# Waiting for the low half in the middle of a product, and joined VectorE operations, in a two-layer transformer block

## The chip, the cores and the metric

The kernel runs on one core of one Trainium2 chip. The metric is the time of one execution on the device in microseconds (us). Before the change the median of three runs was 2668.15 us (2664.14 to 2672.86).

## The reference

The input x has 8 batches of 1024 rows of 256 numbers, all float32. Two blocks follow each other, each behind a layer normalisation that is scaled and shifted per batch (adaLN), and each added back to x with a gate.

```python
h = layernorm(x) * (1 + ca) + sa
x = x + ga * attn(h)          # q, k, v per head group; rope; causal softmax over 1024 rows
h = layernorm(x) * (1 + cb) + sb
x = x + gb * ffn(h)           # two layers:
#   qkv = shift(h) @ wqkv ; q, k = l2norm(q) * qs, l2norm(k) * ks ; rotary + xpos
#   o = local attention: 8 heads of 64, windows of 128 rows, each sees itself and the window before
#   h = h + o @ wo ; n = layernorm(shift(h)) * lg + lb
#   h = h + (a * gelu(g)) @ w2 + b2, with a, g = split(n @ w1 + b1)
```

`shift` moves the second half of the columns down by one row. The rotary step is `t * cos + swap(t) * sin`, where `swap` exchanges the two halves of the 64 columns of a head.

## The kernel before

**Halves.** To keep the accuracy of float32 with float16 products, most operands are stored as a float16 high half and a float16 low half (what is left over). A product is then three matrix products: high times high, high times the other's low, and low times the other's high. The helper `mm3` (lines 160 to 162) issues the three for one block of the contraction: `a[0] b[0]`, `a[0] b[1]`, `a[1] b[0]`. The high half is written by ScalarE (a copy to float16) and the low half after it by VectorE, or by GpSimd for the first normed rows, as the float32 source less the high half.

**Pieces and their order.** The work is cut into pieces, named by a letter or two and numbers for batch or window. A table of planned times (`BEGIN`, `EDGE`, `ONCE`) gives, by sorting, one fixed order of pieces for each engine; the table is not changed. Engines run their own list in order and meet only at semaphores. A piece waits at its start (`wait_ge`) and signals at its end. Every TensorE piece also takes its PSUM banks (`claim`), which waits until the piece that had the bank before is read out. A batch takes about 325 us; the order overlaps the end of one batch's second layer with the start of the next batch's first attention.

**TensorE pieces that the change touches.** `pj` projects 128 normed rows to q, k, v (two blocks of 384 columns, six products, 64 pieces). `sc` forms the causal scores of 128 rows against all rows so far (per bank of 512 columns six products, and one with the mask; 64 pieces). `E` is a third of a window's qkv (six products of 512 columns, 384 pieces). `J` is the output projection of a window (twelve products of 256 columns, 128 pieces). `Wg` and `Wa` are a block of 128 hidden columns for 512 rows, gate and value (six products of 512 columns, 192 and 160 pieces). Each waited at its start for the low half of its rows. The high halves come from ScalarE's pieces `hh` (line 674), `qc` (689), `dh` (723), `nh` (731) and `oh` (809), the low halves from `hl` (GpSimd, line 1316) and VectorE's `ql` (967), `dl` and `nl` (1021) and `ol` (1104). Piece `Y`, the second MLP product, isn't changed: it waits for each block of the hidden rows just before that block's three products.

At the end of a layer the order is: `J` of the last windows, the residual (`jr`, line 1110), the DMA of the rows shifted by one (`xs`), the statistics (1117 to 1122), GpSimd's inverse root (294, 296), the normed rows (1131, 1133), their transposes (407), `nh`, `nl`, and the first `Wg` of those rows.

**VectorE pieces that the change touches.** `rp` (lines 943 to 946) multiplies the q and k columns of a projected tile, read from PSUM, with cos and sin; GpSimd adds the two parts (1321). `x0` and `x1` (1051, 1059) form the cos and sin products of a window's rotary step; GpSimd adds them (1343). `nm` (1084, 1090) takes the inverse of four row sums of the window softmax and scales two of the four heads' probabilities; ScalarE's `na` (791) scales the other two.

Of the kernel before, what the change touches and what calls it, by code (L numbers as in the profile page):

```python
# [18 lines left out]
ALU = mybir.AluOpType  # L19
# [3 lines left out]
P = 128  # L23
EPS = 1e-5
BIG = 1.0e30
BATCH, SEQ, DIM = 8, 1024, 256
NT = SEQ // P
NC = DIM // P
# [3 lines left out]
DEPTH = 2  # L32
HEADS, DH = 8, 64
INNER = HEADS * DH
# [5 lines left out]
HQ = P // 2  # L40
KW = 192
# [5 lines left out]
def adaln_kernel(nc, x, w_q, w_k, w_v, wqkv, q_scale, k_scale, wo, ln_g, ln_b, w1, b1, w2, b2,  # L47
# [3 lines left out]
    with ExitStack() as ctx:  # L51
# [172 lines left out]
        def at(*piece):  # L224

            return rank[piece]
# [61 lines left out]
        def pw_at(f, q, i):  # L288

            return HQ + (HQ + KW) * (4 * f + 2 * q + i)  # L290
# [9 lines left out]
        with block:  # L300
# [100 lines left out]
            def _(pe):  # L401
# [9 lines left out]
                for piece in ORDER["pe"]:  # L411
# [10 lines left out]
                    elif k == "pj":  # L422
                        b, t = ids
                        pe.wait_ge(s_hl, at("hl", b, t // 2))
                        if b == 0 and t == 0:
                            pe.wait_ge(s_bdl, 1)
                        bk = claim(pe, *piece)
                        for c in range(NC):
# [13 lines left out]
                    elif k == "sc":  # L442
                        b, i = ids
                        pe.wait_ge(s_ql, at("ql", b, i))
                        if b == 0 and i == 0:
                            pe.wait_ge(s_masks, 1)
                        bk = claim(pe, *piece)
                        n = (i + 1) * P
                        for kb in range((n + 511) // 512):
                            w = min(512, n - kb * 512)  # L450
                            for c in range(NC):
                                mm3(pe, ps[:, bk + kb, 0:w], [q[:, c, 0, i * P:(i + 1) * P] for q in QK1],
                                    [q[:, c, 1, kb * 512:kb * 512 + w] for q in QK1], c == 0, c == 1)
                        last = pe.matmul(ps[:, bk + i // 4, (i % 4) * P:(i % 4 + 1) * P], id_b[:],
# [32 lines left out]
                    elif k == "E":  # L487
                        n, s = ids
                        L, w = divmod(n, NT)
                        pe.wait_ge(s_dl, at("dl", L, w // 2))  # L490
                        if L < DEPTH and w < 2:
# [3 lines left out]
                        for c in range(NC):  # L495
                            a = w * P + (1 - c)
                            last = mm3(pe, ps[:, bk, :], [q[:, c, a:a + P] for q in ht],
                                       [q[:, L % DEPTH, c, s * INNER:(s + 1) * INNER] for q in wqkv_p], c == 0, c == 1)
                        last.then_inc(s_qkv, 1)
# [68 lines left out]
                    elif k == "J":  # L568
                        n, = ids
                        pe.wait_ge(s_ol, at("ol", n))  # L570
                        if n in (0, NT):
                            pe.wait_ge(s_do, at("do", n // NT))
                        bk = claim(pe, *piece)
                        for c in range(4):
                            last = mm3(pe, ps[:, bk, 0:DIM], [q[:, c, :] for q in ot],
                                       [q[:, n // NT % DEPTH, c, :] for q in wo_p], c == 0, c == 3)
                        last.then_inc(s_wo, 1)
                    elif k in ("Wg", "Wa"):
                        L, g, j = ids
# [8 lines left out]
                        for c in range(NC):  # L588
                            last = mm3(pe, ps[0:m, bk, :], [q[:, L % DEPTH, c, 2 * j + i, 0:m] for q in w1_p],
                                       [q[:, c, a:a + 512] for q in ht], c == 0, c == 1)  # L590
                        last.then_inc(s_w1 if i else s_w1g, 1)
# [293 lines left out]
            def _(dve):  # L885
                for piece in ORDER["dve"]:
# [39 lines left out]
                    elif k == "rp":  # L926
# [6 lines left out]
                        elif b:  # L933
                            dve.wait_ge(s_add, at("ad", last_n(b)))
                        bk = bank["pj", b, t]
                        for c in range(NC):
                            src = ps[:, bk + c, 0:2 * P].rearrange("p (s i e) -> p s i e", s=2, e=2)
                            a = ra[:, t % 2, c].rearrange("p s (i e) -> p s i e", e=2)
                            bb = rb[:, t % 2, c].rearrange("p s (i e) -> p s i e", e=2)
                            cs = cos_t[:, t, c, :].unsqueeze(1).broadcast_to((P, 2, 64))  # L940
                            sn = sin_t[:, t, c, :].unsqueeze(1).broadcast_to((P, 2, 64))
# [90 lines left out]
                    elif k in ("x0", "x1"):  # L1032
# [22 lines left out]
                        if l == 0 and w == 0:  # L1055
                            dve.wait_ge(s_qkt, at("qt", L // DEPTH, NT - 1))
                        for e in range(2):
                            lo, hi = slice(32 * e, 32 * e + 32), slice(32 - 32 * e, 64 - 32 * e)
                            last = dve.tensor_tensor(m2[:, :, :, lo], raw[:, :, :, hi], sn[:, :, :, lo], ALU.mult)  # L1059
                        last.then_inc(s_m, 1)  # L1060
                    elif k == "tm":
# [16 lines left out]
                    elif k == "nm":  # L1078
# [815 lines left out]
```

## Time and profile before

| | |
|---|---|
| median of three runs | 2668.15 us (2664.14 to 2672.86) |
| the profiled execution | 2665.09 us, its span 2663.3 us |
| mean granted TensorE clock | 0.985 |
| TensorE busy | 2533.0 us |
| VectorE busy | 2274.1 us |
| ScalarE busy | 1932.2 us |
| GpSimd busy | 1300.6 us |

The profile comes from one execution. Busy times are the union of an engine's instructions; the ends of matrix products are modelled, so that a product's listed duration is longer than the distance to the next one's start. The distance between starts shows the pace. A wait names the engine whose signal ended it. PE is TensorE, PEld its weight loads, DVE VectorE, ACT ScalarE, POOL GpSimd.

### The profile page before, as it was taken

To read this page: it belongs to the slowest core of one execution; us is meant where nothing else is said; L and a number is where in the kernel's file an instruction comes from. 1 tells how busy PE (TensorE), PEld (TensorE's weight loads), DVE (VectorE), ACT (ScalarE), POOL (GpSimd) and SP (SyncE) were. 2 spreads that over 40 slices of the span, in tenths; PEclk is the share of its full clock that TensorE was granted. 3 is DMA by queue.
4 is the path that set the end of the run, shared out by engine and by line. 5 is a ranking of instruction groups with operands and counts; after the bars stand their busy time and mean duration, and the time that the engine had idled before them with its cause. 6 is when DMAs were issued, how large, how long until landed. Compare 5 with 4: busy or idle time off the path is not lost. (4 is left out here: it accounts for less than half of the span.)

```text
span 2663.3 us, 71937 instructions
## 1 busy us (share of the span) xinstructions
PE 2533.0 (95%) x25566; PEld 1726.5 (65%) x25566; DVE 2274.1 (85%) x6823; ACT 1932.2 (73%) x4782; POOL 1300.6 (49%) x953
## 2 busy tenths in 40 slices
PE   7899989999899998999989999999999999989997
PEld 4566666667566665676656666666766666666675
DVE  8897889878898788987889878898889978799785
ACT  3598856878468784778747787587874888648884
POOL 2364534655355553555435554365544555445552
PEclk7999999999999999999999999999999999999999
DMA  5000010000100000000000000000000000000000
GB/s 190 21 7 8 5 43 2 9 6 8 39 3 9 6 16 30 4 10 4 18 29 5 9 5 20 25 6 8 6 19 25 6 8 6 19 25 6 7 6 21
DMA packets 51026, 46.49 MB, mean 17 GB/s; under 512 B 11530, under 2 KB 47980, under 8 KB 50548
## 3 DMA queue, kind: packets, MB, share of 16 engines
q1 hardware_dynamic: 50004, 40.78, 5.0%
q8 instruction: 213, 3.49, 0.5%
q14 instruction: 137, 1.12, 0.1%
q10 hardware_dynamic: 672, 1.10, 0.1%
HBM read 25.06 MB, written 8.42 MB: 13 GB/s over the span
## 5 line engine op out<-in xcount | busy, mean ns | idle before, releaser
L780 ACT ACTIVATE ar_b<-ar_b,small 128x192 f32<-128x192 f32 (+1 forms) x1024 | 445.3, 437 | 80.7 <-DVE small L1073 79.8
L1343 POOL TENSOR_TENSOR ar_c<-ar_c 128x1024 f32<-128x1024 f32 x128 | 302.7, 2365 | 284.0 <-DVE ar_c L1059 283.2
L1339 POOL TENSOR_TENSOR small<-small,neg_half 128x16 f32<-128x16 f32 x128 | 380.6, 2974 | 115.0 <-DVE small L1031 112.0
L1073 DVE CUSTOM_DVE_ANT_0 ar_b<-ps,mask_t,small 128x192 f32<-128x192 f32 x896 | 318.9, 411 | 27.0 <-PE ps L529 26.8
L1358 POOL TENSOR_TENSOR mlp<-mlp 128x512 f16<-128x512 f32 x160 | 198.0, 1243 | 204.2 <-ACT mlp L835 203.6
L160 PE MATMUL ps<-wqkv_hi,ht_hi 128*128 128x512 f16 x768 | 292.9, 381 | 0.0
L162 PE MATMUL ps<-wqkv_hi,ht_lo 128*128 128x512 f16 x768 | 291.6, 380 | 0.0
L161 PE MATMUL ps<-wqkv_lo,ht_hi 128*128 128x512 f16 x768 | 291.6, 380 | 0.0
L160 PE MATMUL ps<-ht_hi,w_hi 128*128 128x512 f16 (+1 forms) x704 | 269.1, 382 | 11.3 <-DVE ht_lo L1021 11.3
L162 PE MATMUL ps<-ht_hi,w_lo 128*128 128x512 f16 (+1 forms) x704 | 268.3, 381 | 0.0
L161 PE MATMUL ps<-ht_lo,w_hi 128*128 128x512 f16 (+1 forms) x704 | 268.1, 381 | 0.0
L563 PE MATMUL ps<-ar_b,ar_a 128*64 128x128 f32 x3840 | 239.8, 276 | 0.5 <-DVE ar_b L1098 0.3
L294 POOL TENSOR_SCALAR stats<-stats 128x2 f32<-128x2 f32 x128 | 30.4, 237 | 426.6 <-DVE stats L1122 327.7
L563 PEld LDWEIGHTS ps<-ar_b,ar_a 128*64 128x64 f32 x3840 | 207.2, 137 | 30.1 <-issue 20.5
L1149 DVE SCALAR_TENSOR_TENSOR mlp<-ps,bias,mlp 128x512 f32<-128x512 f32 x192 | 142.3, 748 | 75.1 <-PE ps L162 33.7
L529 PE MATMUL ps<-ar_a 64*64 64x64 f32 (+2 forms) x5536 | 196.9, 282 | 2.9 <-ACT ar_a L770 2.8
L791 ACT ACTIVATE ar_b<-ar_b,rsw 128x192 f32<-128x192 f32 (+1 forms) x512 | 192.8, 440 | 7.4 <-DVE rsw L1084 7.1
L780 ACT ACTIVATION_READ_ACCUMULATOR ar_b<-ar_b,small 128x1 f32 x1024 | 193.1, 189 | 0.0
L1098 DVE COPY ar_b<-ps 128x512 f32<-128x512 f32 (+1 forms) x256 | 160.1, 648 | 35.7 <-PE ps L547 35.4
L529 PEld LDWEIGHTS ps<-ar_a 64*64 64x64 f32 x5536 | 153.7, 133 | 40.0 <-issue 22.8
L160 PE MATMUL ps<-w_hi,mlp 128*128 128x256 f16 x640 | 175.3, 274 | 0.2 <-POOL mlp L1358 0.2
L161 PE MATMUL ps<-w_lo,mlp 128*128 128x256 f16 x640 | 175.1, 274 | 0.0
(197 smaller groups left out, 6911.7 us busy)
## 6 DMA issues: line engine op xcount, KB each, us to landing
xu<-in_L_attn_x_dram SPq DMA_DIRECT2D x32, 256.0 KB, 2.9
out_dram<-xu SPq DMA_DIRECT2D x64, 128.0 KB, 2.5
rows<-xu SPq DMA_DIRECT2D x128, 63.5 KB
mlp<-in_L_ffn_wqkv_dram SPq DMA_DIRECT2D x2, 1536.0 KB, 6.6
modb<-mod_rows SPq DMA_DIRECT2D x8, 384.0 KB, 4.3
rows<-in_L_ffn_w_dram SPq DMA_DIRECT2D x2, 1364.0 KB, 10.3
rows<-xu SPq DMA_DIRECT2D x112, 0.5 KB
ar_b<-in_L_wmod_dram SPq DMA_DIRECT2D x2, 768.0 KB, 7.1
```

The source lines that it names most:

```text
L160: pe.matmul(o, a[0], b[0], start=start, stop=False)
L161: pe.matmul(o, a[0], b[1], start=False, stop=False)
L162: return pe.matmul(o, a[1], b[0], start=False, stop=stop)
L529: last = pe.matmul(ps[HQ * half:HQ * half + HQ, bk[q], i * KW + o:i * KW + o + m], QT[r:r + HQ, n % 2, hp, HQ * half:HQ * half + HQ], KT[r ...
L563: last = pe.matmul(ps[64 * q:64 * q + 64, bk, (h // 2) * P:(h // 2 + 1) * P], V[:, (n - 1 + kb) % 4, h * DH:(h + 1) * DH], PTW[:, f, q, 2 ...
L780: last = act.activation(pw, pw, ACT.Exp, bias=mnw[:, n % 2, h:h + 1], scale=-1.0, accum_out=smw[:, n % 2, h:h + 1])
L791: last = act.activation(pw, pw, ACT.Copy, scale=rsw[:, n % 2, h:h + 1])
L1073: last = dve.tensor_tensor_reduce(out=PW[:, pw_at(f, q, i) + c:pw_at(f, q, i) + KW], in0=ps[:, bk, i * KW + c:(i + 1) * KW], in1=mask, sca ...
L1098: dve.tensor_copy(PTW[:, f].rearrange("p x k n -> p (x k) n")[:, c - 1:8:c, 0:HQ], ps[:, bank["H", n, f, 0], :].rearrange("p (k n) -> p k ...
L1339: pool.tensor_tensor(rinv[:, n % 4, :], ssm[:, n % 2, :], neg_half[:, 0:16], ALU.pow).then_inc(s_rinv, 1)
L1343: pool.tensor_tensor(M1[:, n % 2, :], M1[:, n % 2, :], M2, ALU.add).then_inc(s_add, 1)
L1358: pool.tensor_tensor(lo, UB[r, v % 2, :], hi, ALU.subtract).then_inc(s_ul, 1)
```

## The change

In the six kinds of pieces the wait for the low half moves behind the high products, and a wait for the high half stands at the start. The products are the same in number and operands, in another order: first those that need only the high half of the rows, for all blocks of the contraction, then the others. In `pj`, `E`, `J`, `Wg` and `Wa` two thirds of the products come first, in `sc` a third, since there both operands have a late low half.

In VectorE's pieces, operations of one kind on neighbouring parts become one operation with a longer access pattern. `rp` goes from eight operations of 128 elements per partition to three of 256 and two of 128. `x1` goes from two operations of 512 to one of 1024, which reads the halves of each head in swapped order by a negative step. `nm` goes from two operations of 192, each with a per-row scalar (`tensor_scalar`), to one of 384 with the two scalars as a second tensor, repeated by a step of zero (`tensor_tensor`). The regular windows have 192 elements a head, the first window of a sequence 128.

```diff
                     elif k == "pj":
-                        pe.wait_ge(s_hl, at("hl", b, t // 2))
+                        pe.wait_ge(s_hh, at("hh", b, t // 2))
...
                         for c in range(NC):
-                            h = [q[:, c, 1 + t * P:1 + (t + 1) * P] for q in ht]
-                            w = [q[:, c, :, :].rearrange("p s n -> p (s n)") for q in bd_p]
-                            last = mm3(pe, ps[:, bk + c, 0:3 * P], h, w, True, True)
+                            for i in range(2):
+                                pe.matmul(ps[:, bk + c, 0:3 * P], ht[0][:, c, 1 + t * P:1 + (t + 1) * P], w[c][i],
+                                          start=(i == 0), stop=False)
+                        pe.wait_ge(s_hl, at("hl", b, t // 2))
+                        for c in range(NC):
+                            last = pe.matmul(ps[:, bk + c, 0:3 * P], ht[1][:, c, 1 + t * P:1 + (t + 1) * P], w[c][0],
+                                             start=False, stop=True)
                         last.then_inc(s_proj, 1)
...
                     elif k == "sc":
-                        pe.wait_ge(s_ql, at("ql", b, i))
+                        pe.wait_ge(s_qk, at("qc", b, i))
...
+                        for low in range(2):
+                            if low:
+                                pe.wait_ge(s_ql, at("ql", b, i))
+                            for kb in range((n + 511) // 512):
+                                w = min(512, n - kb * 512)
+                                for c in range(NC):
+                                    for q_half, k_half in (((0, 1), (1, 0)) if low else ((0, 0),)):
...
                     elif k == "J":
-                        pe.wait_ge(s_ol, at("ol", n))
+                        pe.wait_ge(s_oh, at("oh", n))
...
                         for c in range(4):
-                            last = mm3(pe, ps[:, bk, 0:DIM], [q[:, c, :] for q in ot],
-                                       [q[:, n // NT % DEPTH, c, :] for q in wo_p], c == 0, c == 3)
+                            for i in range(2):
+                                pe.matmul(ps[:, bk, 0:DIM], ot[0][:, c, :], wo_p[i][:, n // NT % DEPTH, c, :],
+                                          start=(c == 0 and i == 0), stop=False)
+                        pe.wait_ge(s_ol, at("ol", n))
+                        for c in range(4):
+                            last = pe.matmul(ps[:, bk, 0:DIM], ot[1][:, c, :], wo_p[0][:, n // NT % DEPTH, c, :],
+                                             start=False, stop=(c == 3))
...
                     elif k in ("Wg", "Wa"):
-                        pe.wait_ge(s_nl, at("nl", L, 2 * g + 1))
+                        pe.wait_ge(s_nh, at("nh", L, 2 * g + 1))
...
                    elif k == "rp":
...
+                        for e in range(2):
+                            dve.tensor_tensor(a[:, :, :, :, e], src[:, :, :, :, e], cs, ALU.mult)
                         for c in range(NC):
...
-                            for e in range(2):
-                                dve.tensor_tensor(a[:, :, :, e], src[:, :, :, e], cs, ALU.mult)
-                            dve.scalar_tensor_tensor(out=bb[:, :, :, 0], in0=src[:, :, :, 1], scalar=-1.0, in1=sn,
+                            dve.scalar_tensor_tensor(out=bb[:, c, :, :, 0], in0=src[:, c, :, :, 1], scalar=-1.0, in1=sn[:, c],
                                                      op0=ALU.mult, op1=ALU.mult)
-                            last = dve.tensor_tensor(bb[:, :, :, 1], src[:, :, :, 0], sn, ALU.mult)
+                        last = dve.tensor_tensor(bb[:, :, :, :, 1], src[:, :, :, :, 0], sn, ALU.mult)
...
                    elif k in ("x0", "x1"):
...
-                        for e in range(2):
-                            lo, hi = slice(32 * e, 32 * e + 32), slice(32 - 32 * e, 64 - 32 * e)
-                            last = dve.tensor_tensor(m2[:, :, :, lo], raw[:, :, :, hi], sn[:, :, :, lo], ALU.mult)
-                        last.then_inc(s_m, 1)
+                        swap = raw.rearrange("p s h (e d) -> p s h e d", e=2)[:, :, :, ::-1, :]
+                        dve.tensor_tensor(m2.rearrange("p s h (e d) -> p s h e d", e=2), swap,
+                                          sn.rearrange("p s h (e d) -> p s h e d", e=2), ALU.mult).then_inc(s_m, 1)
...
                    elif k == "nm":
...
-                        for i in range(2):
-                            h = 4 * f + 2 * i
-                            pw = PW[:, pw_at(f, 0, i) + c:pw_at(f, 0, i) + KW]
-                            last = dve.tensor_scalar(pw, pw, rsw[:, n % 2, h:h + 1], None, ALU.mult)
-                        last.then_inc(s_pn, 1)
+                        pair = PW[:, pw_at(f, 0, 0) - HQ:pw_at(f, 0, 0) - HQ + 2 * (HQ + KW)].rearrange(
+                            "p (i k) -> p i k", i=2)[:, :, HQ + c:HQ + KW]
+                        scale = rsw[:, n % 2, 4 * f:4 * f + 4:2].unsqueeze(2).broadcast_to((P, 2, KW - c))
+                        dve.tensor_tensor(pair, pair, scale, ALU.mult).then_inc(s_pn, 1)
```

Piece `E` is changed as `J` is, with `dh` and `dl`; `Wg` and `Wa` have the weights on the other side, so their first products are `w1` high and `w1` low times the rows' high half.

## Rows read from the trace of the kernel before

**Rows 1.** The page: busy us (share of span) and instructions; shares of the chain

```profile
PE 2533.0 (95%) x25566; PEld 1726.5 (65%) x25566; DVE 2274.1 (85%) x6823; ACT 1932.2 (73%) x4782; POOL 1300.6 (49%) x953
...
PE 14%; DVE 3%; ACT 2%; issue 1%; DMA 0%; POOL 0%; POOLq 0%; DVEq 0%; ACTq 0%
```

**Rows 2.** Waits of TensorE, whole span: us in total, times, longest us

```profile
PE ps L160 <- POOL ht_lo L1316: 26.0, 17, 5.9
PE ps L160 <- DVE ar_a L967: 23.1, 16, 2.5
PE ps L160 <- DVE rows L1104: 16.7, 16, 1.4
PE ps L160 <- DVE ht_lo L1021: 11.3, 8, 1.4
```

**Rows 3.** The chain at the seam of two batches: start us, us, what

```profile
2289.92 0.70 DVE rows L1104
...
2295.36 0.70 DVE rows L1104
...
2298.09 5.15 DMA rows<-xu
...
2307.45 0.61 ACT ht_hi L731
...
2308.09 0.70 DVE ht_lo L1021
```

**Rows 4.** Timeline of TensorE: start us, us, operation, [idle before, releaser]

```profile
2339.65 0.34 PE L160 MATMUL ps<-ar_a 128*128 128x384 f16 x1 [2.52 <-DVE ar_a L967]
```

**Rows 5.** The chain in the first attention of the last batch

```profile
2328.97 0.40 DVE ar_c L943 x2
2329.37 0.20 DVE ar_c L944
...
2348.68 1.27 POOL ar_c L1321
```

**Rows 6.** Windows: us, busy us (instructions) of each engine, PEclk, DMA share, GB/s

```profile
2326.00:2350.00 24.00, 17.96 (x137) 12.93 (x135) 21.80 (x72) 8.68 (x16) 11.19 (x13) 1.00 0.21 67
...
2430.00:2500.00 70.00, 69.69 (x763) 48.92 (x763) 60.20 (x175) 54.63 (x139) 37.04 (x25) 1.00 0.03 9
...
1366.20:1376.40 10.20, 8.57 (x31) 4.67 (x29) 8.19 (x25) 2.62 (x6) 5.82 (x7) 0.50 0.28 97
```

**Rows 7.** Timeline of TensorE in piece Y, across a wait

```profile
1194.31 0.27 PE L162 MATMUL ps<-w_hi,mlp 128*128 128x256 f16 x1
1194.42 0.27 PE L160 MATMUL ps<-w_hi,mlp 128*128 128x256 f16 x1
```

**Rows 8.** Timeline of VectorE, three stretches

```profile
1404.56 1.23 DVE L1051 TENSOR_TENSOR ar_c<-ar_b,xp_t 128x1024 f32<-128x1024 f32 x1
1405.70 1.29 DVE L1059 TENSOR_TENSOR ar_c<-ar_b,xp_t 128x512 f32<-128x512 f32 x2
1406.91 1.28 DVE L974 TENSOR_TENSOR ar_b<-ps,ar_b 128x512 f16<-128x512 f32 x2
...
1502.08 0.55 DVE L1090 TENSOR_SCALAR ar_b<-ar_b,rsw 128x192 f32<-128x192 f32 x2
1502.54 0.42 DVE L1110 TENSOR_TENSOR xu<-ps,xu 128x256 f32<-128x256 f32 x1
...
1514.97 0.41 DVE L1110 TENSOR_TENSOR xu<-ps,xu 128x256 f32<-128x256 f32 x1
1515.30 1.28 DVE L1059 TENSOR_TENSOR ar_c<-ar_b,xp_t 128x512 f32<-128x512 f32 x2
```

**Rows 9.** Line 1090 alone: duration ns min/median/max, starts, forms

```profile
L1090 DVE TENSOR_SCALAR ar_b<-ar_b,rsw x512: 278/315/1194, 124.8 to 2614.0; 128x192 f32<-128x192 f32 x149, 128x128 f32<-128x128 f32 x22
```

More of the change, by code:

```diff
@@ L427, in _ @@
                         bk = claim(pe, *piece)
+                        w = [[q[:, c, :, :].rearrange("p s n -> p (s n)") for q in bd_p] for c in range(NC)]
                         for c in range(NC):
-                            h = [q[:, c, 1 + t * P:1 + (t + 1) * P] for q in ht]
-                            w = [q[:, c, :, :].rearrange("p s n -> p (s n)") for q in bd_p]
-                            last = mm3(pe, ps[:, bk + c, 0:3 * P], h, w, True, True)
+                            for i in range(2):
[5 more added lines that the diff above has]
+                                             start=False, stop=True)
                         last.then_inc(s_proj, 1)
@@ L448, in _ @@
                         n = (i + 1) * P
[L449 to L453, printed above, removed]
+                        for low in range(2):
[5 more added lines that the diff above has]
+                                    for q_half, k_half in (((0, 1), (1, 0)) if low else ((0, 0),)):
+                                        pe.matmul(ps[:, bk + kb, 0:w], QK1[q_half][:, c, 0, i * P:(i + 1) * P],
+                                                  QK1[k_half][:, c, 1, kb * 512:kb * 512 + w],
+                                                  start=(not low and c == 0), stop=(c == 1 and q_half == 1))
                         last = pe.matmul(ps[:, bk + i // 4, (i % 4) * P:(i % 4 + 1) * P], id_b[:],
@@ L489, in _ @@
                         L, w = divmod(n, NT)
-                        pe.wait_ge(s_dl, at("dl", L, w // 2))
+                        pe.wait_ge(s_dh, at("dh", L, w // 2))
                         if L < DEPTH and w < 2:
@@ L496, in _ @@
                             a = w * P + (1 - c)
-                            last = mm3(pe, ps[:, bk, :], [q[:, c, a:a + P] for q in ht],
-                                       [q[:, L % DEPTH, c, s * INNER:(s + 1) * INNER] for q in wqkv_p], c == 0, c == 1)
+                            for i in range(2):
+                                pe.matmul(ps[:, bk, :], ht[0][:, c, a:a + P],
+                                          wqkv_p[i][:, L % DEPTH, c, s * INNER:(s + 1) * INNER],
+                                          start=(c == 0 and i == 0), stop=False)
+                        pe.wait_ge(s_dl, at("dl", L, w // 2))
+                        for c in range(NC):
+                            a = w * P + (1 - c)
+                            last = pe.matmul(ps[:, bk, :], ht[1][:, c, a:a + P],
+                                             wqkv_p[0][:, L % DEPTH, c, s * INNER:(s + 1) * INNER],
+                                             start=False, stop=(c == 1))
                         last.then_inc(s_qkv, 1)
@@ L574, in _ @@
                         for c in range(4):
-                            last = mm3(pe, ps[:, bk, 0:DIM], [q[:, c, :] for q in ot],
-                                       [q[:, n // NT % DEPTH, c, :] for q in wo_p], c == 0, c == 3)
+                            for i in range(2):
+                                pe.matmul(ps[:, bk, 0:DIM], ot[0][:, c, :], wo_p[i][:, n // NT % DEPTH, c, :],
+                                          start=(c == 0 and i == 0), stop=False)
+                        pe.wait_ge(s_ol, at("ol", n))
+                        for c in range(4):
+                            last = pe.matmul(ps[:, bk, 0:DIM], ot[1][:, c, :], wo_p[0][:, n // NT % DEPTH, c, :],
+                                             start=False, stop=(c == 3))
                         last.then_inc(s_wo, 1)
@@ L588, in _ @@
                         for c in range(NC):
-                            last = mm3(pe, ps[0:m, bk, :], [q[:, L % DEPTH, c, 2 * j + i, 0:m] for q in w1_p],
-                                       [q[:, c, a:a + 512] for q in ht], c == 0, c == 1)
+                            for q in w1_p:
+                                pe.matmul(ps[0:m, bk, :], q[:, L % DEPTH, c, 2 * j + i, 0:m], ht[0][:, c, a:a + 512],
+                                          start=(c == 0 and q is w1_p[0]), stop=False)
+                        pe.wait_ge(s_nl, at("nl", L, 2 * g + 1))
+                        for c in range(NC):
+                            last = pe.matmul(ps[0:m, bk, :], w1_p[0][:, L % DEPTH, c, 2 * j + i, 0:m], ht[1][:, c, a:a + 512],
+                                             start=False, stop=(c == 1))
                         last.then_inc(s_w1 if i else s_w1g, 1)
```

10 lines of the change are left out of this document (5 added, 5 removed).

## The prediction

> **What bounds the kernel now.** I read the shares first: TensorE is busy 95% of the span and VectorE 85% [rows 1], so at most some 130 us of TensorE idleness can be won. The chain of waits comes next. It could be followed over the last 550 us, the last 21% of the span: 14 points of it are TensorE, 3 VectorE, 2 ScalarE [rows 1]. TensorE's own waits say what its idle time waited for, and the four longest are the four kinds of low half that the change moves: 26.0 us for GpSimd's `ht_lo`, 23.1 for `ar_a` (q and k of the first attention), 16.7 for `rows` (the window attention's output), 11.3 for `ht_lo` by VectorE, together 77.1 us [rows 2]. So the question is which of these are on the path that sets the end.
>
> Their counts fit a batch: 16 waits for `rows` are two in each of 8 batches, 8 waits for VectorE's `ht_lo` one each. The chain shows where these three stand, at the seam between two batches [rows 3]: at 2289.92 and 2295.36 it goes from ScalarE's high half of the output through VectorE's subtraction (0.70) into piece J, then through the 5.15 us of the shifted rows' DMA, and at 2307.45 from ScalarE's high half of the normed rows (0.61) through VectorE's subtraction (0.70) into the first Wg. Three times a batch, then, the low half is on the path and TensorE has nothing else in its queue that may go ahead.
>
> The other two kinds stand elsewhere. TensorE sits idle 2.52 us before a score piece at 2339.65 [rows 4], but there the chain runs on VectorE: the rotations from 2328.97 on are on it, and those whose sum GpSimd forms at 2348.68 [rows 5], and from 2326 to 2350 VectorE is busy 21.80 of 24 us against 17.96 for TensorE [rows 6]. In the middle of a batch nothing is idle: TensorE 69.69 of 70 us from 2430 to 2500 [rows 6].
>
> **The waits moved.** A piece that waited for the low half now waits for the high half, sends its high products and waits then. It wins the least of three: the wait itself, the time between the two halves, and the time of the products that go first. For J, eight of twelve products come first; products of 256 columns start 0.11 us apart [rows 7], so 0.87 us. For Wg they are four of six at 0.22 us, 0.86 us. Both exceed the subtraction of 0.70 plus its two hand-overs of some 0.02, so 0.72 is won whole, and the high half, made by ScalarE, is late next. The waits leave room for it: 11.3/8 = 1.41 us for Wg and 16.7/16 = 1.04 for J [rows 2], counted from the end of the product before, which the profile sets at 0.27 us though the next could start after 0.11 [rows 7], so another 0.16 is hidden in it. 3 x 0.72 x 8 batches = 17.3 us, all on the path.
>
> For pj, four of six products come first, 0.16 us each, 0.65 us; for a score piece only two of six (high times high), 0.33 us at the 384 columns of the longer wait; the other of the two waits per batch is 23.1/8 - 2.52 = 0.37 us. That is 17 x 0.65 + 8 x 0.33 + 8 x 0.37 = 17 us of TensorE's idle time, but it lies where VectorE sets the pace (or, for the pj at the seam, in front of the Wg whose high half comes no sooner for it). It returns as a longer wait for VectorE: I take 0, and up to 17 if VectorE isn't the bound there. The E, Wa and J pieces of the middle have waits too short for the list; TensorE is idle 0.31 us in 70 there [rows 6], so 8 batches hold under 8 us, and I take 1.
>
> What a wait in mid-product costs is seen in piece Y, which waits for each block of the hidden rows between two products: L162 at 1194.31, the wait, L160 at 1194.42, 0.11 us like everywhere [rows 7]. A wait already met costs nothing there. So the 992 waits that are added (64 pj, 64 sc, 384 E, 128 J, 352 Wg and Wa) are worth 0; the upper bound is a weight load exposed at each, 1726.5/25566 = 0.068 us [rows 1], 67 us. Behind a mid-product wait that is not met stands all of TensorE's queue, but it stood behind the same wait before, one piece earlier: no start moves back. Products, weight loads and bank claims stay the same in number.
>
> **The joined VectorE operations.** A rotation tile (64 of them) has eight operations of 128 elements, now five. Half of them take 0.80 us on the chain (0.40 for two, 0.20 for the third, as much for the fourth) [rows 5]; one of 256 elements out of PSUM takes 0.33 (L1110 at 1514.97 to the next start) [rows 8]. Three pairs at 0.40 become three at 0.33 to 0.34, so 0.19 a tile, 12 us of VectorE time. Four of a batch's eight tiles are on the chain (two around 2328.97, one ahead of 2348.68, one later; rows 5 show one half tile of the four); the others run beside stretches of the chain on TensorE and GpSimd. 4 x 0.19 x 8 = 6 us. Bounds: 0 and 12.
>
> The swapped halves (128 tiles): two operations of 512 take 1.21 us (1405.70 to 1406.91), one of 1024 takes 1.14 (1404.56 to 1405.70) [rows 8]: 0.07 x 128 = 9 us of VectorE time. VectorE has 3 of the chain's 21 points [rows 1], which gives 1.3 us; I take 1.3. Nothing in the trace reads with a negative step; if it ran at half rate, 1.07 x 128 = 137 us more.
>
> The normalisation (256 pairs): the two `TENSOR_SCALAR` of 192 elements take 0.46 us (1502.08 to 1502.54) [rows 8], 0.23 each. A two-tensor operation of 384 elements lies between 256 (0.33) and 512 (0.60) in rows 8, at 0.47. That is no gain although an operation falls away: I take 0, between -2 (128-wide tiles of the first windows) and +5. The reason is in the numbers: the two-tensor forms cost (0.60 - 0.33)/256 = 1.05 ns an element and 0.06 us fixed, by which 192 elements would take 0.26; the one-source form takes 0.23. The Trainium skill has the rule for it ("VectorE: DVE Perf Modes", section "Mode 2x_2P"): a one-source fp32 operation in SBUF may use both read ports and give two results a cycle, and a `tensor_tensor` cannot. The trace agrees in direction, 0.23 against 0.26. By the count of operations alone, without that rule, the joined form would save 0.06 x 256 = 15 us of VectorE time.
>
> The longest of these operations took 1.19 us, the median one 0.315 [rows 9], so some of them are held up. I put 0 on this, since the joined operation starts where the first of the pair did. The Trainium skill ("SBUF — State Buffer", section "Who interferes with whom") says that both forms, the two-port one and the one with two SBUF inputs, block against a GpSimd operation that reads SBUF; by it nothing changes but the length of the hold.
>
> **Sum.** 17.3 + 1 + 6 + 1.3 + 0 = 25.6 us. The profiled execution took 2665.1 us (its span is 2663.3), so 2639.5; the median of the runs shown, 2668.15, is 3.1 us above the profiled one, and on that scale I predict 2642.5.
>
> **The rivals.**
> (a) More than that. VectorE's relief (12 + 9 us) is all on the path and part of the 17 us of pj and scores comes through: 17 + 21 + 5 = 43 us, 2625. For it: VectorE is busy 21.80 of 24 us at the seam. Against it: half of the rotations are off the chain.
> (b) Given back. The three on-path savings are 5 us apart; if the shifted DMA or ScalarE's order holds one of the three and the rotations' gain goes into GpSimd's add (1.27 us, on the chain behind them), 12 us remain: 2656. For it: VectorE is busy there nearly throughout, and may be late next. Against it: the chain at the seam is serial, and each link waits for the one before.
> (c) The change doesn't shorten anything: a PSUM group left open in mid-product holds back what ran ahead before, or the next semaphore is late by as much. 0 us, 2668. Piece Y speaks against it.
> (d) Slower, by TensorE's clock. It is at half (0.50, the 1.2 GHz level) for 10.2 us from 1366.2, in the first attention of a batch, and at full speed in the middle of the last one [rows 6]. If the changed rhythm of short and split waits brings such a stretch to every batch where TensorE sets the pace, it costs 5.1 x 8 = 41 us: 2642 + 41 = 2683. It decides from 26 us on, that is from 6.5 us at half clock a batch. Against it: the waits get shorter, so TensorE is denser.
>
> **Chances.** Forecast 0.56 (its own range 2634 to 2650), (a) 0.12, (b) 0.15, (c) 0.09, (d) with a slow negative step or exposed weight loads beside it 0.08. A measurement of this kernel tells about 0.3%, 8 us, from no change. Faster by more than that: 0.56 + 0.12 + 0.14 = 0.82; same 0.10; slower 0.08. The range 2628 to 2661 leaves out about a tenth on either side.
>
> **What would show it.** In the changed profile: TensorE's wait for `rows` falls from 16.7 us towards 5 and turns into one for ScalarE's `rows`; the wait for VectorE's `ht_lo` falls from 11.3 by 5.8; those for `ht_lo` by GpSimd and for `ar_a` shrink, with idle time of about that size found elsewhere at the seam. Each seam gets some 3 us shorter, the middle keeps its length. VectorE's busy time falls by some 20 us, from the rotations and the swap and not from the normalisation, whose joined form shows 0.47 us to the next start. TensorE's busy time stays. I am wrong if the middle of a batch changes length, if a met mid-product wait shows a gap over 0.11 or 0.22 us, or if the seam does not shrink.

## The result, and the profile after

The changed kernel takes 2640.14 us (median of four runs, 2639.26 to 2644.93) against 2668.15 for the kernel before (2664.14 to 2672.86): ratio 0.990, 95% interval 0.9883 to 0.9917. That is 28.0 us less, with 25.6 predicted (2642.5 us). One run of the kernel before (2960.05 us) and the one profiled run of `order` (2949.09 us, mean granted clock 0.841) fell into a slower state and are left out of every comparison. Timed again beside its parts, the same change gave 0.9896 (0.9884 to 0.9909), 27 us. The profiled execution took 2644.93 us, span 2642.6, mean granted clock 0.983.

The page of the kernel after, busy us (share) and instructions:

```profile
PE 2536.8 (96%) x25566; PEld 1729.8 (65%) x25566; DVE 2258.1 (85%) x6247; ACT 1932.7 (73%) x4782; POOL 1303.9 (49%) x953
```

VectorE is busy 16.0 us less than in [rows 1], TensorE as before. TensorE's waits after (us in total, times, longest us), for [rows 2]:

```profile
PE ps L419 <- DVE ar_c L936: 12.8, 16, 4.1
PE ps L407 <- DVE rows L1159: 12.6, 16, 5.1
PE ps L461 <- DVE ar_a L995: 10.0, 8, 1.3
PE ps L431 <- ACT ht_hi L702: 9.1, 9, 4.7
PE ps L594 <- ACT rows L837: 5.6, 8, 0.7
PE ps L613 <- ACT ht_hi L759: 5.5, 8, 0.7
PE ps L461 <- ACT ar_a L717: 4.8, 7, 0.7
PE ps L565 <- DVE ar_b L1117: 4.8, 8, 0.6
...
PE ps L435 <- POOL ht_lo L1342: 3.9, 10, 0.8
```

`rows` went from 16.7 us to 5.6 and is now ScalarE's (line 837, before 809): 8 waits instead of 16. `ht_lo` of the first `Wg` (11.3) became ScalarE's `ht_hi` (5.5). The 26.0 for GpSimd's `ht_lo` became 9.1 and 3.9, the 23.1 for `ar_a` 10.0 and 4.8. In their place the transposes of normed rows (lines 419, 407) wait longer. And there is a new one: 0.6 us, eight times, for `ar_b` of line 1117, the normalisation that the change joins (`jw`, where it is not joined, has the same wait). These timelines of the last seam show where it stands. TensorE after (start us, us, operation, [idle before, releaser]), with J of window 14 at 2273.69 between the transposes `H` (line 565) and J of window 15 at 2279.08:

```profile
2273.03 0.71 PE L565 MATMUL ps<-id_f,ar_b 64*128 64x64 f32 x16
2273.69 0.28 PE L594 MATMUL ps<-wo_hi,rows 128*128 128x256 f16 x1
...
2275.77 0.71 PE L565 MATMUL ps<-id_f,ar_b 64*128 64x64 f32 x16 [0.60 <-DVE ar_b L1117]
...
2279.08 0.28 PE L594 MATMUL ps<-wo_hi,rows 128*128 128x256 f16 x1 [0.70 <-ACT rows L837]
...
2291.30 0.39 PE L613 MATMUL ps<-ht_hi,w_hi 128*128 128x512 f16 x1 [0.69 <-ACT ht_hi L759]
```

The same pieces before (the transposes `H` are line 547 there, J and `Wg` line 160):

```profile
2289.29 0.71 PE L547 MATMUL ps<-id_f,ar_b 64*128 64x64 f32 x16
2290.67 0.28 PE L160 MATMUL ps<-wo_hi,rows 128*128 128x256 f16 x1 [0.67 <-DVE rows L1104]
...
2292.08 0.71 PE L547 MATMUL ps<-id_f,ar_b 64*128 64x64 f32 x16
...
2296.11 0.28 PE L160 MATMUL ps<-wo_hi,rows 128*128 128x256 f16 x1 [1.42 <-DVE rows L1104]
...
2308.83 0.39 PE L160 MATMUL ps<-ht_hi,w_hi 128*128 128x512 f16 x1 [1.42 <-DVE ht_lo L1021]
```

VectorE after, same stretch, with the first rotation tile behind it:

```profile
2273.67 0.69 DVE L1130 TENSOR_TENSOR rows<-ps,rows 128x512 f16<-128x512 f32 x1 [0.49 <-ACT rows L837]
2274.54 0.18 DVE L1111 RECIPROCAL rsw<-small 128x4 f32<-128x4 f32 x1 [0.18 <-ACT ar_b L808]
2274.75 0.56 DVE L1117 TENSOR_TENSOR ar_b<-ar_b,rsw 128x384 f32<-128x384 f32 x1
2275.22 0.68 DVE L1124 COPY ar_b<-ps 128x512 f32<-128x512 f32 x1
...
2291.88 0.75 DVE L970 TENSOR_TENSOR ar_c<-ps,cos_t 128x256 f32<-128x256 f32 x2
2292.54 0.48 DVE L972 SCALAR_TENSOR_TENSOR ar_c<-ps,sin_t 128x128 f32<-128x128 f32 x2
2292.94 0.42 DVE L974 TENSOR_TENSOR ar_c<-ps,sin_t 128x256 f32<-128x256 f32 x1
2293.27 0.75 DVE L970 TENSOR_TENSOR ar_c<-ps,cos_t 128x256 f32<-128x256 f32 x2
```

GpSimd of the kernel after, and then the same two operations before (line 1342 is 1316 there):

```profile
2286.66 1.09 POOL L1342 TENSOR_TENSOR ht_lo<-ar_c,ht_hi 128x512 f16<-128x512 f32 x1 [4.86 <-ACT ht_hi L702]
2287.72 0.22 POOL L294 TENSOR_SCALAR stats<-stats 128x2 f32<-128x2 f32 x1
```

```profile
2302.97 1.09 POOL L1316 TENSOR_TENSOR ht_lo<-ar_c,ht_hi 128x512 f16<-128x512 f32 x1 [4.86 <-ACT ht_hi L674]
2304.54 0.22 POOL L294 TENSOR_SCALAR stats<-stats 128x2 f32<-128x2 f32 x1 [0.48 <-DVE stats L1122]
```

How the three savings of a seam fare. J of window 14 sends its high products 0.72 us sooner (1.38 us after the first `H` before, 0.66 now), but the second `H` behind it then waits 0.60 for the normalisation, which VectorE does only after the low half (2273.67) and, from 2274.54, behind ScalarE's exponential: from `H` to `H` it takes 2.79 us before and 2.74 after, so hardly anything passes. J of window 15 gains 0.72 (4.03 us behind `H` before, 3.31 now). Of this 0.2 is lost at the root (line 294): before, GpSimd sat idle 0.48 ahead of it; now `ht_lo` of the next batch stands in front and ends as the root starts. The first `Wg` passes its gain whole: from J of window 15 to it 12.72 us became 12.22, that is its 0.72 less the 0.2.

The windows of the kernel after, its middle and a stretch of the first attention (us, busy us and instructions of PE, PEld, DVE, ACT, POOL, PEclk, DMA share, GB/s), for the last two of [rows 6]:

```profile
2409.00:2479.00 70.00, 69.71 (x795) 49.93 (x794) 60.48 (x165) 55.51 (x145) 37.14 (x24) 1.00 0.04 10
2002.60:2009.40 6.80, 6.11 (x21) 3.31 (x20) 6.20 (x18) 2.52 (x6) 3.56 (x6) 0.50 0.23 81
```

The middle is as dense as before, and half clock still comes in the first attention.

To place the time I cut each batch at ScalarE's operations, which have the same number in every kernel: A, first attention, from the first copy of v to the last exponential; B to the output of window 5; C to window 13; D to the last `nh`; S to the next copy of v. Means over batches 2 to 7 in us, worked out from the traces; "half" is the time at a granted clock of 0.50, per batch.

```
kernel       A     B     C      D     S     sum     half in A   half in D, S
before      61.94 97.58 127.78 31.77 5.05  324.12   5.1         0.6
changed     60.72 97.52 127.73 31.21 4.05  321.23   5.1         0      (run "both")
waits       61.33 97.60 127.63 31.23 4.05  321.83   6.3         0
no_qkv      61.28 97.63 127.70 31.21 4.05  321.87   5.7         0
jw          62.57 97.63 127.69 31.21 4.05  323.15   7.4         0
pjsc        61.39 97.62 127.80 31.79 5.68  324.30   5.1         2.3
joins       61.26 97.54 128.37 31.79 5.33  324.29   2.8         1.1
nm_apart    60.86 97.34 127.74 31.22 4.05  321.21   5.7         0
waits_rp    61.08 97.79 127.64 31.24 4.05  321.80   6.8         0
order_swap  61.47 97.53 127.74 31.64 4.05  322.43   5.7         0
```

D and S together give 1.56 us a batch, A gives 1.22, B and C 0.1. Eight times that is 23.1 us; the first batch gives 1.3 more, which makes the 24.3 between the two profiled executions (2665.09 and 2640.79). The medians are 27 apart. S is 4.77 before in all but one batch; in that one (6.45) 3.4 us of it are at half clock. So 0.28 of the 1.56 is clock, and 1.28 is the moved waits.

The lengths at half clock differ between batches of one kernel, so means of A mix them. Batch by batch, A of the kernel before takes 60.9 us with no half clock, 61.8 with 3.4 us of it, 61.9 to 62.0 with 6.8 and 63.2 with 10.2; A of the changed kernel takes 60.5 with 3.4 and, but for one batch of 61.4, 60.9 to 61.0 with 6.8. The gain of A is therefore 1.0 to 1.3 us at like clock too.

### The profile page after: what moved, and what is told of

Same layout as the page of the kernel before. It is cut to its first block and busy times, and to the rows that moved or that the text cites. A ratio compares the mean times of both kernels' runs of the same rounds, so it can differ in the third digit from the quotient of the medians.

```text
span 2642.6 us, 71361 instructions
## 1 busy us (share of the span) xinstructions
PE 2536.8 (96%) x25566; PEld 1729.8 (65%) x25566; DVE 2258.1 (85%) x6247; ACT 1932.7 (73%) x4782; POOL 1303.9 (49%) x953
## 5 line engine op out<-in xcount | busy, mean ns | idle before, releaser
L514 PE MATMUL ps<-wqkv_hi,ht_lo 128*128 128x512 f16 x768 | 229.0, 380 | 0.0
L617 PE MATMUL ps<-ht_lo,w_hi 128*128 128x512 f16 (+1 forms) x704 | 210.0, 380 | 0.0
L160 PE MATMUL ps<-w_hi,mlp 128*128 128x256 f16 x640 | 174.7, 273 | 0.2 <-POOL mlp L1384 0.2
L162 PE MATMUL ps<-w_hi,mlp 128*128 128x256 f16 x640 | 174.5, 273 | 0.0
## 6 DMA issues: line engine op xcount, KB each, us to landing
rows<-xu SPq DMA_DIRECT2D x128, 63.5 KB
```

The costliest lines, as they stand in the source:

```text
L514: last = pe.matmul(ps[:, bk, :], ht[1][:, c, a:a + P], wqkv_p[0][:, L % DEPTH, c, s * INNER:(s + 1) * INNER], start=False, stop=(c == 1))
L617: last = pe.matmul(ps[0:m, bk, :], w1_p[0][:, L % DEPTH, c, 2 * j + i, 0:m], ht[1][:, c, a:a + 512], start=False, stop=(c == 1))
```

## The experiments

Each was timed in five rounds; ratios are to the kernel before, with 95% intervals.

**both**: the whole change again, as the yardstick for its parts.

> The whole change again, timed beside its parts. Theory S (the seam's chain, with TensorE's low-half waits on it, sets the gain): about 26 us faster than before, 2641 us, ratio 0.990. Theory V (VectorE's saved 20 us carry the gain) and theory C (stretches of TensorE at half clock that come and go) give the same number here; C expects runs that differ by several us from each other with the half-clock stretches that they hold.

2640.92 us, 0.9896 (0.9884 to 0.9909). The result repeats.

**waits**: only TensorE's waits moved, VectorE as before.

```diff
 (pj, sc, E, J, Wg, Wa as in the change; rp, x1, nm as before)
```

> Only TensorE's waits are moved (pj, sc, E, J, Wg, Wa); VectorE's operations stay apart. Theory S: two thirds of the gain or more, 16 to 20 us faster, 2649 us. By the changed profile each seam passes on only 1.3 of the 2.17 us that were predicted, so with 0.3 us from each middle some 13 us is the low end. Theory V: at most 5 us faster.

2647.47 us, 0.9924 (0.9912 to 0.9936): 20 of the 27 us.

**joins**: only the joined operations.

```diff
 (rp, x1, nm as in the change; all TensorE pieces as before)
```

> Only VectorE's operations are joined (rp, x1, nm); all TensorE waits stay as before. Theory S: 6 to 8 us faster, 2660 us (0.21 us for each of the four rotations per batch on the chain, and little from the swap and the normalisation). Theory V: 20 us faster, 2648.

2665.91 us, 0.9997 (0.9988 to 1.0005): a miss for both theories. Alone they gain 0.7 us a batch in A (0.1 to 0.4 where the time at half clock is alike: 60.47 against 60.87 with none) and lose 0.6 in C and 0.3 in S. S's loss is clock, in two batches instead of one; in the others S is 4.77 as before. C's loss comes at one spot of each batch. VectorE and GpSimd of `joins` (nm is line 1089):

```profile
1834.78 0.56 DVE L1089 TENSOR_TENSOR ar_b<-ar_b,rsw 128x384 f32<-128x384 f32 x1
...
1836.62 0.35 DVE L1129 TENSOR_SCALAR rows<-xu,stats 128x128 f32<-128x128 f32 x1 [0.61 <-POOL stats L296]
```

```profile
1834.79 0.62 POOL L294 TENSOR_SCALAR stats<-stats 128x2 f32<-128x2 f32 x1 [9.11 <-DVE stats L1120]
1835.50 1.09 POOL L296 TENSOR_TENSOR stats<-stats,neg_half 128x2 f32<-128x2 f32 x1
```

And of the kernel before, VectorE, then GpSimd:

```profile
1835.28 0.57 DVE L1090 TENSOR_SCALAR ar_b<-ar_b,rsw 128x192 f32<-128x192 f32 x2
...
1836.60 0.35 DVE L1131 TENSOR_SCALAR rows<-xu,stats 128x128 f32<-128x128 f32 x1
```

```profile
1835.30 0.22 POOL L294 TENSOR_SCALAR stats<-stats 128x2 f32<-128x2 f32 x1 [9.11 <-DVE stats L1122]
1835.60 0.96 POOL L296 TENSOR_TENSOR stats<-stats,neg_half 128x2 f32<-128x2 f32 x1
```

Both times GpSimd's root starts with VectorE's normalisation. Beside the one-source form it takes 0.22 us, beside the joined one 0.62, and the 0.5 us by which `joins` was ahead is gone when the normed rows start (1836.62 against 1836.60). Behind the normed rows VectorE forms the low half of a J, and this J, which starts on the low half, now waits for it (TensorE of `joins`):

```profile
1838.39 0.28 PE L160 MATMUL ps<-wo_hi,rows 128*128 128x256 f16 x1 [0.51 <-DVE rows L1102]
```

Such a root of over 0.6 us stands at the same spot in seven batches (2 to 8), and TensorE's waits for `rows` rise from 16 [rows 2] to 23:

```profile
PE ps L160 <- DVE rows L1102: 20.4, 23, 1.4
```

The changed kernel has the same seven long roots, but there the J sends its high products meanwhile and doesn't wait, and C takes no longer (127.73, with nm apart 127.74). So some 4 us (0.6 us in seven batches) of what the joined operations give beside the moved waits are lost where they stand alone. The longest operations of line 294 agree, in `before` and then in `joins` (ns min/median/max):

```profile
L294 POOL TENSOR_SCALAR stats<-stats x128: 213/219/381, 5.1 to 2627.3; 128x2 f32<-128x2 f32 x128
```

```profile
L294 POOL TENSOR_SCALAR stats<-stats x128: 217/219/625, 5.0 to 2628.9; 128x2 f32<-128x2 f32 x128
```

It is 627 in the changed kernel and 381 in `nm_apart`: over 0.6 us only where nm is joined.

**jw**: only J, Wg and Wa moved.

```diff
 (J, Wg, Wa as in the change; pj, sc, E and VectorE as before)
```

> Only J, Wg and Wa wait in mid-product; pj, sc and E as before, VectorE as before. Theory S: all of what the moved waits give, that is the same as with all six moved, 11 to 18 us faster; the profile shows the seam passing on 0.05 us from the first J, 0.5 from the second and 0.7 from Wg. Rival: the first attention's pj and sc waits carry half of it, then this run gives under 8 us.

2657.41 us, 0.9958 (0.9946 to 0.997): 10 to 11 us, not the 20 of all waits. D and S are those of `waits` to 0.02 us; the difference is A, 62.57 against 61.33. A is even longer than before (61.94), by its longer time at half clock alone: with 3.4 us of it A takes 61.5 to 61.9, with 6.8 61.95, as before or less.

**pjsc**: only pj and sc.

```diff
 (pj, sc as in the change; E, J, Wg, Wa and VectorE as before)
```

> Only pj and sc wait in mid-product. The prediction says 0 us: TensorE's idle time there falls by up to 17 us and returns as other idle time, since VectorE sets the pace (ratio 1.000, within 3 us). Rival: part of the 17 us reaches the end, 5 to 10 us faster.

2665.35 us, 0.9998 (0.999 to 1.0007). The time is the one predicted, but two effects cancel: A is 0.55 us a batch shorter (0.3 to 0.7 between batches with a like time at half clock), and S 0.63 longer, all of it in batches with half clock there. The other runs agree: the mean granted clock is 0.979 to 0.983 in all twelve runs of `pjsc` and 0.983 to 0.989 in the 29 of the kernel before beside it. In `pjsc` the first `Wg` of the last seam (TensorE) runs at half pace, its products 0.43 us apart (2308.26 to 2308.69); before they are 0.22 apart:

```profile
2307.86 0.61 PE L160 MATMUL ps<-ht_hi,w_hi 128*128 128x512 f16 x1 [1.42 <-DVE ht_lo L1031]
2308.26 0.63 PE L161 MATMUL ps<-ht_lo,w_hi 128*128 128x512 f16 x1
2308.69 0.63 PE L162 MATMUL ps<-ht_hi,w_lo 128*128 128x512 f16 x1
```

**no_qkv**: all waits moved but E's.

```diff
 (waits, with E as before)
-                        pe.wait_ge(s_dh, at("dh", L, w // 2))
+                        pe.wait_ge(s_dl, at("dl", L, w // 2))
```

> Before with the waits of pj, sc, J, Wg and Wa moved, and E (the qkv products) left as before; no joined operation. All waits together took 20 us, J, Wg and Wa alone 11 of them, pj and sc alone nothing. Theory: the 9 us between are TensorE's clock in the first attention of a batch, which at half level lasted 10.2 us in four of seven batches where only J, Wg and Wa were moved and 3.4 or 6.8 us where all were, and it is pj's and sc's earlier products, just ahead of that stretch, that shorten it. Expected: 2648 us (0.992 to 0.993), half level of 3.4 or 6.8 us at the first attention in every batch. Rival: it is E that carries the 9 us (its 768 products lie in the middle too, where its wait for the low half stood): 2657 us (0.996), with 10.2 us at half level in about half of the batches.

2646.27 us, 0.992 (0.9905 to 0.9935): as `waits`. So E's wait is worth nothing, and pj and sc, worth nothing alone, bring 10 to 11 us on top of `jw`. A window at half clock in A of `jw`, then of `no_qkv`:

```profile
393.50:403.70 10.20, 8.57 (x30) 4.92 (x31) 8.17 (x26) 2.67 (x7) 5.44 (x6) 0.50 0.22 77
```

```profile
391.20:398.00 6.80, 6.33 (x23) 3.53 (x22) 6.04 (x19) 2.24 (x5) 4.90 (x7) 0.50 0.51 177
```

In `jw` four of batches 2 to 8 have such a stretch of 10.2 us, and their A takes 63.1 to 63.5 us; the three with 3.4 or 6.8 us take 61.5 to 62.0. In `no_qkv` no stretch is over 6.8 us and A takes 60.9 to 61.5. So of the 11 us some 4 to 5 are the products that go first (0.5 us a batch where the clock is alike) and some 6 to 7 the shorter stretches at 1.2 GHz. This comes from one profiled execution of each; the mean granted clock of all five runs of each agrees in direction (0.981 to 0.983 in `jw`, 0.984 to 0.987 in `no_qkv`). Why the stretches are shorter no run shows.

**met_waits**: the kernel before, with waits that are already met between all products of E, J, Wg and Wa.

```diff
             pe.matmul(o, a[0], b[0], start=start, stop=False)
+            met()        # pe.wait_ge on the low half the piece has waited for
             pe.matmul(o, a[0], b[1], start=False, stop=False)
+            met()
```

> The kernel before with the start wait of E, J, Wg and Wa repeated in front of each product that mm3 issues second and third: 5632 waits more, all met already. The prediction says a met wait costs nothing: same as before, 2668, within 3 us. Rival (each holds back the next weight load, 0.068 us): hundreds of us slower; at 0.02 us each still 110 us.

2666.18 us, 0.9996 (0.9988 to 1.0005). By the counts of the profile's page these are (768 + 512 + 704) x 2 = 3968 waits, four times those that the change adds; the 5632 of the expectation is a miscount. A met wait costs nothing that can be measured: the interval's end, 1.3 us, is 0.3 ns a wait.

**nm_apart**: the whole change, with nm's two `tensor_scalar` as before.

```diff
-                        dve.tensor_tensor(pair, pair, scale, ALU.mult).then_inc(s_pn, 1)
+                        for i in range(2):
+                            h = 4 * f + 2 * i
+                            pw = PW[:, pw_at(f, 0, i) + c:pw_at(f, 0, i) + KW]
+                            last = dve.tensor_scalar(pw, pw, rsw[:, n % 2, h:h + 1], None, ALU.mult)
```

> The whole change but for the normalisation, which stays two one-source operations of 192 elements. The prediction says that joining them is worth 0 (0.47 us against 0.46 from start to start): same time as the whole change, 2641 us, within 3. Rival (an operation fewer saves its fixed part): 5 us slower than the whole change, 2646. Opposite rival (the two-tensor form delays GpSimd and the transposes behind it): 3 us faster than the whole change.

2641.88 us, 0.9907 (0.9894 to 0.9919), and 321.21 against 321.23 us a batch: the joined normalisation is worth nothing that can be told from 0 here (1 us by the medians of `both` and this run).

**waits_rp**: all waits, and rp.

```diff
 (waits, with rp as in the change; x1 and nm as before)
```

> All waits moved as in the change, and of the joined operations only rp (the rotations of the first attention). Theory of the prediction: rp stands on the path there and is worth 6 us, x1 1.3 and nm nothing, so that this kernel is at 2641.5 us (0.990), within 1 us of the whole change; the VectorE busy time falls by some 9 us. Rival: of the 6.7 us between the waits alone and the whole change rp has only the 0.4 us a batch that the first attention showed, 3 us, and the rest is x1's (0.2 us a batch in the stage behind, and less load): 2644 us (0.9912). In `joins` nm cost the middle 0.5 us a batch by slowing GpSimd, and here, without nm, the middle should stand at 127.6 us a batch.

2645.41 us, 0.9915 (0.9898 to 0.9931). Against `waits` A is 0.25 us shorter (0.4 in four batches with a like time at half clock) and B 0.19 longer, so rp is worth 0 to 2 us, less than either theory said. C is 127.64, as expected without nm. TensorE's wait for the rotations' sum (line 445, for GpSimd) falls from 6.0 us in `waits` to 5.0, in 8 waits.

From here to `nm_apart` only x1 is added: 3.5 us by the medians, and 0.45 us a batch in B. The intervals of `waits`, `waits_rp`, `nm_apart` and `both` overlap from one to the next, so this split among rp, x1 and nm is likely and not shown; that the three together give some 6.6 us beside the moved waits is shown, since the intervals of `waits` (from 0.9912) and `both` (to 0.9909) don't overlap.

**order**: the whole change, and the order at the end of a layer: the high and low half of window 14 each behind one softmax operation of window 15, J of window 14 behind both transposes.

```diff
 (("oh","act"), ("ol","dve"), ("J","pe"), ("jr","dve"), window 14 only)
-14: 297.22   -14: 297.83   -14: 298.57  -14: 300.08
+14: 297.9    +14: 298.75   +14: 301.0   +14: 301.2
```

> The whole change, and in the table of times at the end of a batch: ScalarE forms the exponentials of the last window's last heads before the high half of the window before (oh 14 behind ex 15,1,0), VectorE normalises them before the low half (ol 14 behind nm 15,1), TensorE runs J 14 behind H 15,1 and I 15,0, and the residual follows. Theory S' (the first J's 0.66 us is lost because the last window's transposes wait 0.60 us for the normalisation, which is queued behind that low half): some 0.4 us a batch faster than the whole change, 3 to 4 us, 2637. Rival (the order is balanced as it is, J 14 now delays the residual and the statistics): same or up to 5 us slower.

2669.05 us, 1.0007 (0.9999 to 1.0016): a miss by some 30 us, and all of the change's gain is gone. The aim was the 0.60 us wait for line 1117.

**order_swap**: of these only the two halves moved, J and jr left.

```diff
 (("oh","act"), ("ol","dve"), window 14 only)
-14: 297.22   -14: 297.83
+14: 297.9    +14: 298.75
```

> The whole change, with only two items of the order moved: at each sequence's last windows the high half oh of window 14 goes behind one softmax exponential on ScalarE, and its low half ol behind the joined normalisation of window 15 on VectorE; TensorE's order is as in the change (J of window 14 between the two transposes H of window 15), which is the half of `order` that J did not take part in. Theory: `order` lost 28 us because TensorE reached H of window 15 without J ahead of it, and waited for the normalisation (14.4 us in all there against 4.8) and because J then stood last in a row behind it; here H's 0.6 us wait per sequence goes and J waits as much longer for the high half, so the time is the whole change's within 3 us: 2638 to 2644 us. Rival: it is the late halves themselves that cost, through the bank and the residual that wait for them: 2655 us or more, as most of the 28 us would be here.

2649.29 us, 0.993 (0.9917 to 0.9944): 8 us over the change, between the two theories (it misses both). The new wait goes, and that for the high half grows from 5.6 us in 8 to

```profile
PE ps L594 <- ACT rows L837: 13.5, 16, 1.0
```

so 7.9 is paid for 4.8, and D is 0.43 us longer. That is 3.4 us in 8 batches. In the profiled execution most of the rest is in A, where one batch has two separate stretches at half clock and takes 64.35 us. The other 20 us of `order` come with J and the residual moved behind the second transpose; their cause stays open, since the trace of `order` can't be set beside the others.

## Why the prediction was right, and where its terms were not

The forecast held: 2640.14 us against 2642.5. That it held so closely is in part luck, since its terms did not: the seams gave 7 us less than forecast, and pj and sc, which were put at 0, some 4 to 5 more, with the clock adding to it.

- **17.3 us at the seams for J and Wg**: 10.2 measured (1.28 x 8). `jw` has the same D and S; that its total is 10 to 11 too is chance, since it loses 0.63 us a batch in A. Wg's 0.72 is exact: S falls from 4.77 to 4.05. Of J's 1.44 only 0.56 comes through (D, 31.77 to 31.21). I asked what is late next for J and answered "the high half, made by ScalarE". For window 14 it is VectorE's normalisation, for the transpose behind J, which has 0.6 us less cover; for window 15 it is a GpSimd operation, now in front of the root. The mean wait of 1.04 us also hid that the two differ (0.67 and 1.42).
- **1 us in the middle**: B and C give 0.1 us a batch, as said.
- **0 us for pj and sc, 17 as the upper bound**: this term was wrong. Some 0.5 us a batch, 4 us in all, comes through in A, in `pjsc` and in `no_qkv` alike. I set it to zero because the chain runs on VectorE there. A chain that alternates between the engines would pass part of it; that this is the reason is argued and not shown.
- **TensorE's clock**: rival (d)'s mechanism exists, but not in the changed kernel, where half clock in A stays at 5.1 us a batch, and its price was too high: 10.2 us at half clock in A of the kernel before cost 2.3 us (63.17 against 60.87 with none), not 5.1. Moving J and Wg alone lengthens the stretches at half clock in A (5.1 to 7.4 us a batch); pj and sc take that back. Moving pj and sc alone puts them on the first Wg. Neither has a cost of its own in the sum. Half clock at the seam (D, S) occurs in one batch of the trace before, where it costs 1.7 us, and in none of the changed kernel's; this was not in my sum.
- **rp 6 us, x1 1.3, nm 0**: 6.6 together (2647.47 less 2640.92) against 7.3 predicted, but probably split otherwise: rp 0 to 2, x1 3 to 4, nm 0 to 1. rp's size is right, 1.39 us from tile to tile (2291.88 to 2293.27) against 1.60 [rows 5]; four tiles a batch on the path was then too many, and x1, counted by VectorE's share of a chain that covers 21% of the span, too little. VectorE's busy time went as forecast for these two, by 10.9 us for rp and 9.0 for x1 (2273.0, 2262.1 and 2253.1 in `waits`, `waits_rp` and `nm_apart`); the joined nm gives 5.1 of it back (2258.2 in `both`), which makes the 16 measured against "some 20".
- **nm's price**: 0.47 us to the next start, as predicted (2274.75 to 2275.22). That the join changes "nothing but the length of the hold" was wrong in one respect. The Trainium skill ("SBUF — State Buffer", section "Who interferes with whom") has both forms block a GpSimd operation in SBUF; here a GpSimd operation beside the pair of `tensor_scalar` took 0.22 us and beside the joined `tensor_tensor` 0.62. For that case the measurement decides: the two forms are not alike, and in `joins` the difference was on the path.
- **Mid-product waits at 0**: confirmed, with four times as many.
- **Rival (b)'s sum** is 2 us off: without one J's 5.8 us and the rotations' 6, 13.8 of the 25.6 remain, not 12.

Of the rivals, (a) is out: the joined operations bring 6.6 us and not 21, though part of pj's and sc's 17 us did come through. (b) was half true: of the three savings at the seam one is held up nearly whole and one in part, and A makes up for it. (c) is excluded by `waits`, and (d) by the changed kernel's clock.

## What to carry to other kernels

Where a product waits for the second of two operands, send what needs only the first and wait in mid-product: the wait is free here, and the gain is at most the shortest of the wait, the operand's delay and the time of the products that go first. Take off what the next piece on the engine then waits, because it lost as much cover: of 0.72 us each, 0.05, 0.5 and 0.72 were left. Follow each saving one piece further, to what stands behind the piece that was sped up. Parts of a change don't add up where the clock or a wait on another engine lies between: here 11 us alone (J, Wg, Wa) and 0 alone (pj, sc) made 20 together, and with another 0 alone (the joined operations) 27.

## What the hardware showed that I had not expected

- In the first attention and at the seam of batches 2 to 8 the stretches at half clock are 3.4, 6.8 or 10.2 us long. Most stand at about the same spot of the first attention, and kernels with small edits elsewhere have them longer or at other places; two executions of the changed kernel differ in one batch (6.8 us against 3.4). By that alone the edit of pj and sc cost 5 us by itself (S, 0.63 us a batch) and brought some 6 to 7 beside that of J and Wg.
- A negative step over SBUF costs a float32 `tensor_tensor` nothing: the joined x1 of 1024 elements has a mean of 1217 to 1237 ns in the changed kernel, and x0, of the same size with no swap, 1226 to 1240.
- GpSimd's `tensor_scalar` of 128x2 (line 294) takes 0.62 us instead of 0.22 in seven of its 128 executions in `both`: those that start 0.01 us after a joined nm, which reads two tensors from SBUF. Beside a VectorE operation with one of its two inputs in PSUM it takes 0.22 (62 executions). At the start of the pair of one-source operations of 192 elements it takes 0.22 too (all seven in `before`, six of seven in `nm_apart`, the other 0.35), and 0.36 to 0.38 when it starts 0.17 us into a `tensor_scalar` of 128x256 (line 936) or a `scalar_tensor_tensor` on SBUF (line 1035).
